# Stage borders of a long fused kernel: one barrier in place of two or more, with the semaphores cleared beside the next stage

## The reference

```python
x = x + _L0_attn_ref(_layernorm(x), ...)   # windowed, 16 heads, with a latent path
x = x + _L0_ffn_ref(_layernorm(x), ...)    # 4-bit quantised feed-forward
x = x + _L1_attn_ref(_layernorm(x), ...)   # full attention, 16 heads
x = x + _L1_ffn_ref(_layernorm(x), ...)    # 8 experts, two of them for each token
x = x + _L2_attn_ref(_layernorm(x), ...)   # causal attention, 16 heads
x = x + _L2_ffn_ref(_layernorm(x), ...)    # two layers of local attention and feed-forward
x = x + _L3_attn_ref(_layernorm(x), ...)   # state space model
x = x + _L3_ffn_ref(_layernorm(x), ...)    # 16 experts, two of them for each token
```

## Time and profile before

| | |
|---|---|
| median of three executions | 2716.77 us |
| the profiled execution | 2713.88 us |
| its span, first to last instruction | 2712.4 us |
| PE (matmul) busy | 2198.8 us, 81% |
| DVE busy | 1877.2 us, 69% |
| ACT busy | 1521.7 us, 56% |
| POOL (GpSimd) busy | 711.6 us, 26% |
| mean granted TensorE clock | 0.890 of full speed |

### The profile page before, as it was taken

One profiled execution on the slowest core, in us unless ns is written; L12 is line 12 of the kernel. 1 busy time (PEld: TensorE's weight loads), 2 busy tenths in 40 slices (PEclk: granted clock), 3 DMA queues, 4 the chain that ended last, 5 costly groups with the idle time before them and its releaser, 6 DMA issues. The chain is left out here.

```text
span 2712.4 us, 58466 instructions
## 1 busy us (share of the span) xinstructions
PE 2198.8 (81%) x22165; PEld 1164.4 (43%) x22194; DVE 1877.2 (69%) x2796; ACT 1521.7 (56%) x3201; POOL 711.6 (26%) x1286
## 2 busy tenths in 40 slices
PE   5975567699999999956766999998679888876678
PEld 2653334133333333236751444444447546645533
DVE  5644765999999999444347887884776495457577
ACT  2552453288888888832331777777367357442321
POOL 3870000000000000004620222222466095204356
PEclk8996787599999999977875999999889999987789
DMA  2320001511211211001113222230110000010000
GB/s 89 84 56 0 10 2 47 120 43 37 52 47 33 53 49 31 4 18 32 43 41 102 61 71 72 59 78 6 48 32 2 13 24 2 1 30 3 1 1 16
DMA packets 71134, 102.61 MB, mean 38 GB/s; under 512 B 26691, under 2 KB 45285, under 8 KB 70858
## 3 DMA queue, kind: packets, MB, share of 16 engines
q1 hardware_dynamic: 58506, 88.12, 12.2%
q10 hardware_dynamic: 9856, 5.64, 1.0%
q0 software_dynamic: 2496, 5.12, 0.7%
HBM read 80.53 MB, written 14.09 MB: 35 GB/s over the span
## 5 line engine op out<-in xcount | busy, mean ns | idle before, releaser
L947 DVE TENSOR_REDUCE l1a_core_mpart<-l1a_core_psA 128x1 f32<-128x1024 f32 x512 | 600.6, 1218 | 41.1 <-PE l1a_core_psA L859 29.3
L929 ACT ACTIVATE l1a_core_prob<-l1a_core_psB 128x512 f32<-128x512 f32 x1024 | 552.0, 596 | 99.6 <-PE l1a_core_psB L874 79.3
L1291 ACT ACTIVATE l2a_core_prob<-l2a_core_psB 128x384 f32<-128x384 f32 (+3 forms) x656 | 303.5, 526 | 135.9 <-PE l2a_core_psB L1229 132.2
L1316 DVE TENSOR_REDUCE l2a_core_mpart<-l2a_core_psA 128x1 f32<-128x1024 f32 (+4 forms) x352 | 290.9, 878 | 43.0 <-PE l2a_core_psA L1211 41.2
L886 PE MATMUL l1a_core_psV<-l1a_core_prob,l1a_core_vh 128*32 128x512 f32 x2048 | 265.6, 594 | 0.2 <-ACT l1a_core_prob L929 0.2
L874 PE MATMUL l1a_core_psB<-l1a_core_qh,l1a_core_kh 75*32 75x512 bf16 x2560 | 195.5, 382 | 0.8 <-ACT l1a_core_prob L929 0.8
L1245 PE MATMUL l2a_core_psV<-l2a_core_prob,l2a_core_vh 128*32 128x256 f32 (+3 forms) x1856 | 168.9, 421 | 0.4
L1156 POOL TENSOR_SCALAR_AFFINE_SELECT l2a_core_prob<-l2a_core_prob 128x128 f32<-128x128 f32 x256 | 73.9, 293 | 316.9 <-ACT l2a_core_prob L1291 313.6
L1229 PE MATMUL l2a_core_psB<-l2a_core_qh,l2a_core_kh 75*32 75x512 bf16 (+3 forms) x1720 | 134.8, 338 | 0.9 <-ACT l2a_core_prob L1291 0.7
L819 POOL CAST l1a_core_mb<-l1a_core_negm 128x16 bf16<-128x16 f32 x16 | 3.1, 197 | 472.9 <-PE l1a_core_psA L859 408.9
L874 PE MATMUL l1a_core_psB<-l1a_first_qh,l1a_first_kh 75*32 75x512 bf16 x1536 | 119.4, 388 | 4.6 <-ACT l1a_core_prob L929 4.6
(11 more groups left out here) (742 smaller groups left out, 4604.6 us busy)
## 6 DMA issues: line engine op xcount, KB each, us to landing
l2f_tab<-in_rotary SPq DMA_DIRECT2D x32, 128.0 KB
l0a_core_qh<-qparts SPq DMA_DIRECT2D x36, 96.0 KB
l0a_core_kh<-kparts SPq DMA_DIRECT2D x36, 96.0 KB
l1a_core_qa<-qparts SPq DMA_DIRECT2D x32, 96.0 KB
l1a_core_ka<-kparts SPq DMA_DIRECT2D x32, 96.0 KB
l2a_core_qa<-qparts SPq DMA_DIRECT2D x32, 96.0 KB
l2a_core_ka<-kparts SPq DMA_DIRECT2D x32, 96.0 KB
l1a_core_qh<-qparts SPq DMA_DIRECT2D x30, 96.0 KB
```

The source lines that it names most:

```text
L929: nc.scalar.activation(prob[u % (2 * PER_KB)][:], psB[u % 3][:], ACT.Exp, scale=scale).then_inc(b_exped, 1)
L947: nc.vector.tensor_reduce(mpart[:, n // 2, n % 2:n % 2 + 1], psA[i % 2][:], AX.X, ALU.max).then_inc(a_freed, 1)
L1291: nc.scalar.activation(prob[n % RING][:, 0:cols], psB[n % 3][:, 0:cols], ACT.Exp, scale=scale).then_inc(b_exped, 1)
L1316: ins = nc.vector.tensor_reduce(mpart[:, place, part:part + 1], psA[i % 2][:, lo * P:hi * P], AX.X, ALU.max)
```

## The change

`close()` no longer has a barrier. GpSimd alone clears the stage's semaphores, behind the barrier of the block that has just ended, and goes on with its work of the next block; the other engines go on at once. The numbers are not freed at the border but when the next block has ended (`Stage.cleared`), so the next stage takes other semaphore numbers. The semaphores on which GpSimd's own DMAs report (`gathered`, `scattered`) are neither cleared nor freed.

```diff
 class Stage:
+    cleared = []
...
-    def sem(self, name):
+    def sem(self, name, of_gpsimd_dma=False):
         s = self.nc.alloc_semaphore(name=f"{self.name}_{name}")
-        self.sems.append(s)
+        if not of_gpsimd_dma:
+            self.sems.append(s)
         return s

+    @contextmanager
     def block(self):
-        return self.nc.Block()
+        with self.nc.Block() as block:
+            yield block
+        for s in itertools.chain(*Stage.cleared):
+            self.nc.release_semaphore(s)
+        Stage.cleared.clear()

     def close(self, *outer):
         outer = [o for o in outer if o]
-        self.nc.clear_and_free_semaphores(self.sems + [s for o in outer for s in o.sems])
-        self.nc.all_engine_barrier()
+        done = sorted(self.sems + [s for o in outer for s in o.sems], key=lambda s: s.num)
+        first = 0
+        for i in range(len(done)):
+            if i + 1 == len(done) or done[i + 1].num != done[i].num + 1:
+                self.nc.gpsimd.sem_clear(range(done[first].num, done[i].num + 1))
+                first = i + 1
+        Stage.cleared.append(done)
         self.ctx.close()
...
-        self.gathered = [self.sem(f"gathered{i}") for i in range(self.AHEAD)]
+        self.gathered = [self.sem(f"gathered{i}", of_gpsimd_dma=True) for i in range(self.AHEAD)]
...
-    scattered = [st.sem(f"scattered{i}") for i in range(NY)]
+    scattered = [st.sem(f"scattered{i}", of_gpsimd_dma=True) for i in range(NY)]
```

More of the change, by code:

```diff
@@ L12 @@
-from contextlib import ExitStack
+import itertools
+from contextlib import ExitStack, contextmanager
 import numpy as np
```

## The result

The changed kernel takes 2672.19 us (median of six executions, 2665.65 to 2678.41), the kernel before 2718.35 us in the same runs (six, 2704.61 to 2722.42). The ratio is 0.9833, with an interval of 0.9817 to 0.9849: faster by 45 us, 41 to 50. The forecast was 2683 us with a range of 2667 to 2701, a gain of 34 us. So the direction and the main term are right, and the gain came out about a third larger. It lies inside the range as a whole, but outside the 2675 to 2692 that rival 1 (*the sum holds*) gave itself; it falls among the times of rival 4, which had a chance of 0.10.

What follows compares the result with a forecast made beforehand. Taken as bound: a chain of 38 stages, with every engine standing still at borders. Borders of 36.2 us, less 2 for GpSimd's clears and 0.5 for transfers, gave 33.7 off 2716.77: 2683 us, range 2667 to 2701.

Steps and rivals of the forecast that it cites:

- rival 1: Whole kernel: the summed gain holds, 2683 us, own range 2675 to 2692; chance 0.68.
- rival 4: Second and third attention cores: clock rises earlier or falls less often, worth 6 to 13 us, 2670 to 2677; chance 0.10.
- Borders: Between blocks at 37 borders: barriers and clears of close() take 36.2 us, with 32.8 as lower reading.
- durations alone: All clears and barriers of close(), counted with no gap between instructions: a floor of 17.5 us, result 2699.
- The split into c and b: At borders with close(): c, a barrier, costs 0.24 us; b, a clear, costs 0.16 us.
- No cost for entering a block: Start of each block: nothing added for entering after one barrier, engines starting about 0.1 us after the release.
- Rival 3: Block starts: the border hides loading of the next block's instructions, so no change, 2716 us; chance 0.04.
- I took 2 us: Mainly three attention cores: first matmuls wait for GpSimd's clears, 1 to 3 us; other first work 0 to 1 us.
- Rival 2: Block starts nearly everywhere: engines wait for GpSimd's first product behind its clears, 2697 to 2705 us; chance 0.08.
- The 0.5 us for transfers already under way: Start of l1e: gathered rows issued in the stage before are still awaited, eating 0.5 us of the gain.
- TensorE's clock: Whole kernel: the one thing that could add or take more than the sum; left to rivals, up to 0.63 us per low-level microsecond.
- the sum's sign in the profile: All stages of the changed kernel: each keeps its length, the long ones too.

Runs made afterwards that it cites:

- the eightfold clears: The changed kernel with each clear issued eight times on GpSimd: ratio 0.9871 against the kernel before.
- two opposite experiments: Five barriers added at three borders of the changed kernel: 0.9891; four matmuls added at each close() of a stage with a bank, in the kernel before: 1.0002.

## Why the prediction was right, and where its size was off

**Borders: right.** 36.2 us stood between the blocks and all of it is gone. Two profiles of the kernel before and three of the changed one agree on this to 0.1 us, and putting the barrier back brings 22 of them back and 28 us in time. The bound "durations alone", 17.5 us, was far off, as the gaps between sequencer instructions are as long as the instructions.

**The split into c and b: half right.** I solved for 0.24 us a barrier and 0.16 us a clear from times read to 0.1 us. The barrier behind a clear is 0.25 us (22.4 us less 99 × 0.10, over 51), but one by itself 0.36 to 0.41. The clear was 0.16 us only because of its DRAIN; 0.10 without. The sum did not rest on the split.

**No cost for entering a block: right.** At every border of the changed kernel the first instruction behind the release starts within 0.12 us, as at the one border with a single barrier, and in the kernel before too. Rival 3 is out. The Trainium skill (Runtime: NRT & Kernel Launch, Instruction fetch mechanics) has a stall for a taken branch to code that is not loaded; no border of this kernel shows one.

**GpSimd: right in place, too large in price.** I took 2 us. The three first matmuls are 0.21 us late each, 0.6 us in all, since a clear lost its DRAIN and two remain at each of these borders. The clears on ScalarE give just that back. Rival 2 is out by the eightfold clears. The 0.5 us for transfers already under way is not seen in the total. Together these two terms were some 2 us too large.

**The term that was mis-sized is TensorE's clock.** I gave it no part in the sum ("the rows show no border at which this decides") and put it in rival 4 with 0.10. What the gain has beyond the borders is about 9 us, 45 measured less 36; that it is the clock is shown for 3.5 to 4 us of it. I had looked for it at the starts of the long cores, where nothing was gained (l1a_core 697.2 and 697.3 before, 698.1 after, at 0.96 in each). What is shown was at short borders behind busy stages. At l3f_out PE's idle time fell from 2.26 to 0.94 us and the granted clock, which had been at 1.2 GHz for the whole stage, stayed at 2.4. The row was there before: a line of PE's order of time with 16 matmuls of 128 columns at 3.64 us. The Trainium skill (TensorE: Matmul & The Clock Gate, Why this matters for your kernels) says that gaps between bursts should be kept short. The trace agrees in that, but the gaps of 1.92 to 2.26 us behind which the clock was low here are shorter than the one that the page warns of, and in the kernel with the barrier put back a gap of 1.90 us did not bring it down. I had cited the page for a rival where it was a term.

The price was wrong too. Rival 4 took 0.63 us for each microsecond at the low level, from a stretch full of matmuls; over whole executions it is 0.25 to 0.34. And what I had named as the sum's sign in the profile, that each stage keeps its length, failed both ways: three stages are 1.1 to 1.7 us shorter each time, while l1r is 2.1 to 2.3 us longer. The lower end of rival 1's own range, 2675, has no term behind it either; 5 us of scatter give 2678.

**What stays open.** The clock's part is shown, by two opposite experiments, for l3f_out and the two l2f norms, 3.5 to 4 us together. l3c, 1.8 to 2.1 us shorter in the changed kernel, does not follow its border: it takes 66.5 us with the barrier doubled and 68.8 us with it put back once. That the rest of the 9 us is the clock as well is argued from the mean clocks and from the doubled barrier (8 us beside 18 us of borders), not shown, and the matmuls at the borders speak against idle time at the borders as its whole cause. Low stretches also move from one stage to the next, as at l2f ffn and l1r, so the stages don't add up neatly in single profiles.

## What to carry to other kernels

Read a staged kernel once by its borders: the time between the last release of one block and the first work of the next is in no busy share, yet here it was 36 us in 2712. Clearing semaphores needs no barrier of its own if the numbers are not used again until the next block's barrier has passed; one engine with slack can do it beside the work. And idle time of TensorE can cost more than its length: where a border is cut, look at the duration of the first matmuls behind it, for they tell whether the clock had fallen.

## What the runs showed of the hardware

- A barrier of five engines costs 0.25 us behind a semaphore clear and 0.36 us by itself (18.3 us for 51); a range clear 0.10 us (1.45 us for 14 of them), or by the two borders of the earlier trace rows 0.16 us with its DRAIN.
- The same 16 matmuls took 3.64 us behind 2.26 us of idle time and 1.94 us behind 0.94 us, at a granted clock of 0.50 and 1.00. With the barrier put back they took 1.94 us at 1.00 behind 1.90 us. Four short matmuls, 0.38 us of work in the gap, also went with a clock that stayed up.
- Chips differ in one place: the experts of layer 1, with their gathers and scatters of rows, took 144 to 146 us on the first chip and 128 to 130 us on the other two, in every version of the kernel. That is most of the 16 to 20 us between the medians of the kernel before. Which part of the stage is slower there was not settled.
